# A GRU over 200 steps: gathers of 127 rows with single-row fetches beside them, and a softmax for each chain

## What is computed

```python
x = emb[item_seq]                     # 512 x 200 x 128, f32
def step(h, (x_t, m_t)):              # 200 steps
    mx = x_t @ W + b_i                # 128 -> 3*128
    mh = h @ U + b_r
    z = sigmoid(mx[:, :D] + mh[:, :D])
    r = sigmoid(mx[:, D:2*D] + mh[:, D:2*D])
    hh = tanh(mx[:, 2*D:] + r * mh[:, 2*D:])
    return where(m_t, z * h + (1 - z) * hh, h)
out = softmax(h_last @ Wout + bout)
```

## Time and profile before

| | us |
|---|---|
| median of 3 runs | 1042.61 (1042.57 to 1042.8) |
| profiled execution: span | 1043.0 |
| profiled execution: its own time | 1044.85 |
| PE, DVE, ACT, POOL busy | 975.0, 794.0, 593.0, 765.2 |
| table gathers, L356: count, mean | 738, 0.946 |
| single-row DMAs, L275: count | 1792 |

### The profile page before, as it was taken

One profiled execution on the slowest core, in us unless ns is written; L12 is line 12 of the kernel. 1 busy time (PEld: TensorE's weight loads), 2 busy tenths in 40 slices (PEclk: granted clock), 3 DMA queues, 4 the chain that ended last, 5 costly groups with the idle time before them and its releaser, 6 DMA issues.

```text
span 1043.0 us, 20057 instructions
## 1 busy us (share of the span) xinstructions
PE 975.0 (93%) x5201; PEld 758.8 (73%) x5201; DVE 794.0 (76%) x2074; ACT 593.0 (57%) x1292; POOL 765.2 (73%) x807
## 2 busy tenths in 40 slices
PE   6899999999999999999999999898888988989885
PEld 4556888777777777777777777676666766767664
DVE  3344667888888888888888888777777777777775
ACT  2334555666666666666666666555555555555553
POOL 6576777777777777777777777777777777777772
PEclk9999999999999999999999999999999999999998
DMA  9999555555555555555555555555555555555552
GB/s 357 404 355 282 162 162 159 160 163 160 162 161 160 160 160 161 161 162 161 159 162 159 161 161 161 160 159 162 159 161 162 159 159 161 159 161 160 162 160 71
DMA packets 63942, 184.75 MB, mean 177 GB/s; under 512 B 18207, under 2 KB 21577, under 8 KB 63914
## 3 DMA queue, kind: packets, MB, share of 16 engines
q0 software_dynamic: 48768, 148.29, 50.4%
q1 hardware_dynamic: 13750, 35.24, 9.1%
q10 hardware_dynamic: 1396, 0.91, 0.3%
HBM read 158.31 MB, written 26.08 MB: 177 GB/s over the span
## 4 chain that ended last, share of the span: by engine, by line
PE 53%; POOL 28%; issue 10%; DVE 3%; DMA 3%; ACT 2%; SPq 1%; DVEq 0%; POOLq 0%; ACTq 0%
POOL arena L356 28%; PE bank L443 13%; PE bank L449 9%; PE bank L445 9%; PE bank L431 8%; PE bank L372 5%; PE bank L437 4%; DMA rows<-turned 2%; PE bank L412 1%; PE bank L413 1%; PE bank L417 1%; ACT cand L547 1%; DVE h L610 1%; DVE rh L605 1%; DVE pre L614 1%
## 5 line engine op out<-in xcount | busy, mean ns | idle before, releaser
L356 POOL DMA_INDIRECT arena<-table,row_table x738 | 698.0, 946 | 228.1 <-issue 220.4
L545 ACT ACTIVATE bank<-bank,b_gates 128x256 f32<-128x256 f32 x400 | 179.2, 448 | 252.4 <-PE bank L449 252.4
L431 PE MATMUL bank<-ident,arena 128*128 128x128 f32 x1504 | 254.4, 278 | 44.4 <-DMA arena<-table,row_table 42.7
L431 PEld LDWEIGHTS bank<-ident,arena 128*128 128x128 f32 x1504 | 185.8, 141 | 113.2 <-DMA arena<-table,row_table 74.9
L443 PE MATMUL bank<-h,U_sb 128*128 128x256 f32 x800 | 264.6, 412 | 1.1 <-DVE h L610 1.1
L620 DVE SCALAR_TENSOR_TENSOR bank<-bank,cand 128x256 f32<-128x256 f32 x400 | 172.8, 432 | 121.4 <-ACT cand L547 118.7
L547 ACT ACTIVATE cand<-pre,bi 128x256 f32<-128x256 f32 x400 | 202.9, 507 | 85.9 <-DVE pre L614 85.9
L449 PE MATMUL bank<-h,U_sb 128*128 128x256 f32 x800 | 240.5, 383 | 0.0
L605 DVE SCALAR_TENSOR_TENSOR rh<-bank,br,r 128x256 f32<-128x256 f32 x400 | 193.4, 484 | 60.2 <-ACT r L543 53.2
L445 PE MATMUL bank<-h,U_sb 128*128 128x256 f32 x800 | 238.4, 380 | 0.0
L543 ACT ACTIVATE r<-bank,b_gates 128x256 f32<-128x256 f32 x400 | 189.7, 474 | 36.4 <-PE bank L443 31.9
(11 more groups left out here) (58 smaller groups left out, 236.3 us busy)
## 6 DMA issues: line engine op xcount, KB each, us to landing
arena<-table SPq DMA_DIRECT2D x1792, 1.5 KB
table<-proj SPq DMA_DIRECT2D x24, 768.0 KB, 4.0
arena<-table,row_table POOLq DMA_INDIRECT x738, 3.1
arena<-in_L_rec_emb SPq DMA_DIRECT2D x12, 512.0 KB, 9.9
rows<-turned SPq DMA_DIRECT2D x12, 512.0 KB, 10.2
raw<-rows,row_table POOLq DMA_INDIRECT x48, 4.3
seq<-in_r_item_seq ACTq DMA_DIRECT2D x1, 400.0 KB, 8.0
table<-proj SPq DMA_DIRECT2D x2, 192.0 KB
```

Source lines behind the costliest of these rows:

```text
L356: pool.indirect_dma_start(ring_rows(s, k), None, table, bass.IndirectOffsetOnAxis(row_table[:, t, k:k + 1], 0)).then_inc(s_slot[s][k], 16)
L431: pe.matmul(dst[:, i * P:(i + 1) * P], ring_row(s, k, g), ident[:, :], start=(i == 0), stop=False, is_transpose=True, skip_group_check=True)
L545: act.activation(update_sum[c], update_sum[c], ACT.Sigmoid, bias=b_gates[:, 0:1]).then_inc(s_z[c], 1)
```

## The change

There are two parts. **The gathers.** POOL now gathers all 56 blocks of a turn, but of each only the rows of partitions 0 to 126 (752 gathers of 127 rows instead of 738 of 128). SP fetches the row of partition 127 of each block and step with a DMA of its own, four for each step: 752 single-row DMAs instead of 1792. Their offsets need no way through DRAM any more: POOL writes `row_offsets` for all steps and blocks, and SP loads the 28 of half a turn from partition 127 of it. SP waits for both chains to free the slot. PE waits, before the first transpose of each chain, for the four rows of the step as well (`s_last_row[s]`). The raw gathers stay at 128 rows. **The softmax.** It runs for each chain by itself: the bias is added by PE (identity times `bout_sb`, ahead of the wait for h), DVE takes the negated maximum of a chain, ACT computes exp with it as bias and adds up the total as it goes, one instruction per block, DVE inverts and multiplies, and SP stores the two halves apart.

```diff
-            def slow_block(turn):
-                for first in range(0, P, BATCH_ROWS):
...
-                        if isinstance(turn, int):
-                            sp.wait_ge(s_slot[SLOW_STEP][SLOW_BLOCK], 16)
-                        else:
-                            sp.wait_ge(s_free[1], (turn - 1) * RING + SLOW_STEP + 1)
-                    for i in range(BATCH_ROWS):
-                        p = first + i
-                        sp.dma_start(slot[p:p + 1, :], table_bytes[:, bass.ds(offset[i], ROW_BYTES)]
-                                     ).then_inc(s_slow, 16)
+            def last_rows(turn, steps):
+                for half in range(2):
+                    n = steps // 2
                     _, offset = nc.values_load_multi_w_load_instructions(
...
+                        row_offsets[P - 1:P, bass.ds((turn * RING + half * n) * BLOCKS, n * BLOCKS)],
...
+                    for i in range(n):
+                        s = half * n + i
+                        if not isinstance(turn, int) or turn > 0:
+                            for c in BOTH:
+                                sp.wait_ge(s_free[c], (turn - 1) * RING + s + 1)
+                        for k in range(BLOCKS):
+                            sp.dma_start(ring_rows(s, k)[P - 1:P, :].bitcast(U8),
+                                         table_bytes[:, bass.ds(offset[i * BLOCKS + k], ROW_BYTES)]
+                                         ).then_inc(s_last_row[s], 16)
...
                     for k in CHAINS[c]:
-                        if (s, k) == (SLOW_STEP, SLOW_BLOCK):
-                            continue
                         if n < RAW:
                             pool.wait_ge(s_slot[n][k], 16)
                         pool.indirect_dma_start(
-                            ring_rows(s, k), None, table,
-                            bass.IndirectOffsetOnAxis(row_table[:, t, k:k + 1], 0)
+                            ring_rows(s, k)[0:P - 1, :], None, table,
+                            bass.IndirectOffsetOnAxis(row_table[0:P - 1, t, k:k + 1], 0)
                         ).then_inc(s_slot[s][k], 16)
...
-                        if n == 0 and (s, k) == (SLOW_STEP, SLOW_BLOCK):
-                            pe.wait_ge(s_slow, (turn + 1) * (P * 16))
-                        elif n == 0:
+                        if n == 0:
+                            if i == 0:
+                                pe.wait_ge(s_last_row[s], (turn + 1) * (BLOCKS * 16))
                             pe.wait_ge(s_slot[s][k], turn * 16 + (32 if s < RAW else 16))
...
             for c in BOTH:
+                for i in range(2):
+                    pe.matmul(logits[c][:, i * CLASSES:(i + 1) * CLASSES], ident[:, :], bout_sb[:, :],
+                              start=(i == 0), stop=False, skip_group_check=True)
                 pe.wait_ge(s_h[c], STEPS + 1)
...
+            for c in BOTH:
+                act.wait_ge(s_top[c], 1)
+                for i, k in enumerate(CHAINS[c]):
+                    act.activation(exps[:, k, :], logits[c][:, i * CLASSES:(i + 1) * CLASSES], ACT.Exp,
+                                   bias=minus_top[:, k:k + 1], accum_out=total[:, k:k + 1]).then_inc(s_exp[c], 1)
...
+            for c in BOTH:
+                first, end = CHAINS[c][0], CHAINS[c][-1] + 1
+                dve.wait_ge(s_logit_ps[c], 1)
+                dve.tensor_reduce(minus_top[:, first:end], logits[c].rearrange("p (k n) -> p k n", k=2),
+                                  AX.X, ALU.max, negate=True).then_inc(s_top[c], 1)
+            for c in BOTH:
+                first, end = CHAINS[c][0], CHAINS[c][-1] + 1
+                dve.wait_ge(s_exp[c], 2)
+                dve.reciprocal(inv_total[:, first:end], total[:, first:end]).then_inc(s_inv[c], 1)
+                dve.wait_ge(s_inv[c], 1)
+                dve.tensor_tensor(probs[:, first:end, :], exps[:, first:end, :],
+                                  inv_total[:, first:end].unsqueeze(2).to_broadcast([P, 2, CLASSES]), ALU.mult
+                                  ).then_inc(s_prob[c], 1)
```

More of the change, by code:

```diff
@@ L53, in gru @@
     LEFT = STEPS - RAW - TURNS * RING
-    assert SLOW_STEP < min(RAW, LEFT)
+    assert RING % 2 == 0 and LEFT % 2 == 0 and RING * BLOCKS // 2 <= 32
     BOTH = range(len(CHAINS))
@@ L112, in gru @@
         row_table = sb("row_table", [P, STEPS, BLOCKS], I32)
-        slow_offsets = sb("slow_offsets", [P, TURNS + 1], I32)
-        slow_line = sb("slow_line", [1, (TURNS + 1) * P], I32)
+        row_offsets = sb("row_offsets", [P, (STEPS - RAW) * BLOCKS], I32)
         copy_i = sb("copy_i", [P, 1], I32)
@@ L135, in gru @@
         zh = chain_tiles("zh")
-        logits = sb("logits", [P, BLOCKS, CLASSES])
         exps = sb("exps", [P, BLOCKS, CLASSES])
-        top = sb("top", [P, BLOCKS])
+        probs = sb("probs", [P, BLOCKS, CLASSES])
+        minus_top = sb("minus_top", [P, BLOCKS])
         total = sb("total", [P, BLOCKS])
@@ L148, in gru @@
         x_sum = [bank[4 * c + 3][:, 0:WIDTH] for c in BOTH]
-        logit_bank = bank[3]
+        logits = [bank[4 * c + 3][:, 0:2 * CLASSES] for c in BOTH]
         turn_bank = bank[0:4]
@@ L176, in gru @@
         s_slot = [[sem(f"slot{s}_block{k}_gathered") for k in range(BLOCKS)] for s in range(RING)]
[L177 to L180, removed]
+        s_offsets = sem("row_offsets_ready")
+        s_last_row = [sem(f"slot{s}_last_rows_fetched") for s in range(RING)]
         s_x = per_chain("x_turned")
@@ L194, in gru @@
         s_h = per_chain("h_ready")
[L195 to L198, removed]
+        s_logit_ps = per_chain("logits_summed")
+        s_top = per_chain("tops_ready")
+        s_exp = per_chain("exp_ready")
+        s_inv = per_chain("totals_inverted")
+        s_prob = per_chain("probs_ready")
         s_out = sem("out_stored")
@@ L245, in _ @@
             sp.dma_start(table[ITEMS + 1:ITEMS + 1 + P, :], last[:, 2, :]).then_inc(s_last, 16)
[L249 to L254, removed]
             for q in range(AHEAD):
@@ L257, in _ @@
             sp.wait_ge(s_padrow, 16 * 2)
-            sp.wait_ge(s_slow_line, 16)
-            slot = ring_rows(SLOW_STEP, SLOW_BLOCK).bitcast(U8)
-            def slow_block(turn):
-                for first in range(0, P, BATCH_ROWS):
+            sp.wait_ge(s_offsets, 1)
+            def last_rows(turn, steps):
+                for half in range(2):
+                    n = steps // 2
                     _, offset = nc.values_load_multi_w_load_instructions(
-                        slow_line[0:1, bass.ds(turn * P + first, BATCH_ROWS)], engines=[sp.engine],
-                        min_val=0, max_val=(ITEMS + P) * ROW_BYTES,
+                        row_offsets[P - 1:P, bass.ds((turn * RING + half * n) * BLOCKS, n * BLOCKS)],
+                        engines=[sp.engine], min_val=0, max_val=(ITEMS + P) * ROW_BYTES,
@@ L286, in _ @@
+            last_rows(0, RING)
+            with sp.Fori(1, TURNS) as turn:
+                last_rows(turn, RING)
+            last_rows(TURNS, LEFT)
+            for c in BOTH:
+                first, end = CHAINS[c][0], CHAINS[c][-1] + 1
+                sp.wait_ge(s_prob[c], 1)
+                sp.dma_start(out[first * P:end * P, :].rearrange("(k p) n -> p k n", p=P),
+                             probs[:, first:end, :]).then_inc(s_out, 16)
+            sp.wait_ge(s_out, 16 * len(CHAINS))
         @block.gpsimd
@@ L323, in _ @@
             pool.wait_ge(s_idx, 7)
-            pool.tensor_scalar(slow_offsets[:, :], row_f[:, SLOW_BLOCK, RAW + SLOW_STEP:STEPS:RING],
+            pool.tensor_scalar(row_offsets[:, :].rearrange("p (t k) -> p t k", k=BLOCKS),
+                               row_f.rearrange("p k t -> p t k")[:, RAW:STEPS, :],
                                float(ROW_BYTES), None, ALU.mult).then_inc(s_offsets, 1)
@@ L495, in _ @@
             for c in BOTH:
+                for i in range(2):
+                    pe.matmul(logits[c][:, i * CLASSES:(i + 1) * CLASSES], ident[:, :], bout_sb[:, :],
+                              start=(i == 0), stop=False, skip_group_check=True)
                 pe.wait_ge(s_h[c], STEPS + 1)
[L497 to L501, removed]
+                for i in range(2):
+                    last = pe.matmul(logits[c][:, i * CLASSES:(i + 1) * CLASSES], h[c][:, i * P:(i + 1) * P],
+                                     Wout_sb[:, :], start=False, stop=True, skip_group_check=True)
+                last.then_inc(s_logit_ps[c], 1)
         @block.scalar
@@ L563, in _ @@
             over_table_steps(act, one_turn)
-            act.wait_ge(s_soft, 3)
-            act.activation(exps[:, :, :], logits[:, :, :], ACT.Exp).then_inc(s_exp, 1)
+            for c in BOTH:
[3 more added lines that the diff above has]
+                                   bias=minus_top[:, k:k + 1], accum_out=total[:, k:k + 1]).then_inc(s_exp[c], 1)
         @block.vector
```

5 lines of the change are left out of this document (removed).

## The result

The changed kernel takes **2260.88 us** (median of 4 runs, 2260.15 to 2262.68) where the kernel before takes 1042.7: a ratio of 2.168, 95% interval 2.165 to 2.171. The forecast was 996.4, the range 990 to 1060. The direction and the size are both wrong.

A forecast was written before the change was run, and what follows sets the result against it. The prediction took POOL's gather stream to bound the kernel before, and PE the changed one: 1043.0 - 44.2 (PE's pace) - 2.0 (softmax) = 996.8 us of span, less 0.4 = 996.4 us; range 990 to 1060.

The forecast's parts named there:

- What bounds the kernel: PE sets the pace until about 640 us, then POOL's gather stream does, 1.2507 us from start to start.
- D: Forecast case: gathers get cheap enough that PE's own pace bounds the kernel, 996.4 us; chance 59%.
- rival B: Gathers on one engine at unchanged generation cost, the longer landing on the path: 1063 to 1068 us; chance 7%.
- Part 1: One more POOL gather per turn, 752 for 738: 17.5 us at the old price, all on the path.
- the offsets' way through DRAM: SP's two offset DMAs through DRAM go; SP had time there, gain 0.
- Part 2: POOL's gathers of 127 rows for 128: generation below 0.87 us, bounds 0.06 to 0.939 us, far end 1.21.
- Part 3: With PE as the bound at 2.186 us per slot, the span falls by 44.2 us to 998.8.
- the 44 us: Span saved once PE's own pace sets the end: 44.2 us.
- SP's single rows and the added wait: SP's row fetches cost 0; PE's new waits per step taken as 0, kept at 0 to 8 us.
- POOL's larger table of offsets: Table grown to 128x752 elements takes 1.6 to 2.9 us, hidden behind 9.55 us of POOL idling: cost 0.
- Part 4: Softmax per chain after the last h: 1.7 us left of 3.80, gain 2.0 us, 1.6 if the sum lengthens exp.
- A: Cost is per row or engines stay sixteen; POOL remains the bound: 1052.6 to 1058.1 us; chance 20%.

The follow-up runs named there:

- 112-row run: The changed kernel with 112 rows instead of 127 in POOL's gathers, SP's single rows and the waits kept, rows 112 to 126 left out: 1038.22 us, ratio 0.9961.
- the ladder: The changed kernel without SP's fetches and PE's wait for them, POOL's gathers at another row count each turn, from 128 to 32: 1303.4 us.

## Why the prediction was wrong

**What bounds the kernel: right for the kernel before, wrong for the changed one.** I had PE take over (D); POOL's stream stayed the bound. From the first table gather to the last plus a tail it gave every span that I computed within 1%, except that of the 112-row run (1.2%). With the measured 2.845 us from start to start, the forecast's own sum for POOL, 102.86 + 751 x 2.845 + 16.4, is 2255.9 us, 2266 with rival B's 10 us for the longer landing; the span was 2260.8.

**Part 1, right in kind, less in size.** I said 17.5 us for the 14 gathers. The runs with all 128 rows and with the softmax alone differ by just this part of the change: 1054.16 - 1039.94 = 14.2 us, 14.0 in the two profiled spans. Three things take the 17.5 down. The fourteenth gather is that of the very last block, behind the gather that PE waits for last (the seventh before the last with the softmax alone, the eighth with all 128 rows), so only 13 gathers lengthen the path: 1.25 us less, a mistake of my sum. POOL's pace up to that gather was 1.2500 us and not 1.2519: 1.4 us. And 1.5 us is that the first table gather starts earlier (100.95 against 102.49 us); the gather waited for last landed 0.7 us later instead. The earlier start is the item that I had costed at nothing: the offsets' way through DRAM. In the three kernels that keep it the first table gather starts at 102.5 to 103.2 us, in the five without it at 100.3 to 101.0. In the three POOL waits there for the table's stores, 2.2 to 3.7 us. That the way through DRAM delays the end of these stores, by its 1,792 pieces of 4 B, is argued and not shown.

**Part 2 is the step that failed, and the whole of the error.** I took two shares of a gather's 0.946 us that could shrink, per row and per engine, and concluded that one engine instead of sixteen can only make it cheaper. The bounds ran from 0.06 to 0.946 us, with 1.21 as a remote end. The true cost is a third thing, the waves: n/k times an entry for *all* sixteen engines. I had the right fact in hand, that 127 divides by nothing, and the right consequence for the transfer: one engine per gather, landing at "about 13 us", measured 12.8. But the same packets of the earlier trace rows fit "eight waves of sixteen" just as well as "sixteen engines of eight rows", and nothing in them excluded that the number of waves, which goes from 8 to 127, carries the price. The upper bound of an operation that the trace does not show was set where the known form stands; a form that splits differently could cost more, and I gave that no row and no chance. The 119 further waves cost 119 x 13.1 ns = 1.56 us and the step from k = 16 to k = 1 another 0.03: 1.60 us per gather, 1.2 ms in all. My sentence on the Trainium skill's rule ("DMA: Bandwidth & Descriptors", "Why a DMA increments its semaphore by 16 and not by 1") had a hint at the missing half: from GpSimd all 16 engines post the semaphore whatever the shape. I read it as "the cost per engine might stay", never as "times the waves".

**Part 3.** PE's pace without POOL as the bound was not tested; the 44 us stayed unreached. The parts costed at nothing held: SP's single rows and the added wait (112 rows against 128: 15.9 us measured, 15.8 from the gathers alone), and POOL's larger table of offsets (2.78 us in the ladder, behind which POOL still idles 5.5 us).

**Part 4.** 2.0 us said, 2.0 measured on the chain from h to the last product, plus 0.8 for the halved store, which I had missed. The reading of the sum, 0.19 us, is real; the first of chain 1's lies beside the second exp, the second stands in front of the reciprocal. The terms were off and made up for each other, which is luck: chain 1's two exps with their readings took 0.76 us (0.34 for an exp) where I had 0.54, and the gaps 0.09 where I had 0.25.

**The rivals.** A had the engine that bounds and the sign, but its price stopped at today's. B was the nearest: one engine, long landing, on the path. It kept 0.946 us for the generation. None of the rivals let the generation grow.

## What to carry to other kernels

The number of rows of an indirect gather is a shape, and its price follows n/k, with k the largest divisor of n up to 16. Keep it a multiple of 16; one row less can cost more than twice. And when a trace does not show a form of an operation, bound its cost on both sides by how the work would be *divided*, not only by how much of it there is: fewer engines can mean more steps. Taking rows off a gather that keeps k = 16 brings little, since by the ladder 0.84 of its 0.947 us do not depend on them (0.865 us at 32 rows, less two waves; 112 rows save 21 ns).

## What the runs showed of the hardware that I had not expected

- A wave of a gather costs POOL 13.1 ns for k under 16 and 0.873 us stand beside it; at k = 16 the same 8 waves are 33 ns cheaper than at k = 15 (0.947 against 0.980 us).
- With k = 1, the fifteen engines without a row are still given some 4 B per row: 530,944 packets in the queue instead of 48,768.
- Landing grows with the rows and the bytes of the one engine: 12.7 us for 127 rows of 1,536 B, 7.4 for 127 of 512 B, 7.6 for 61 of 1,536 B, against 3.1 for 128 rows on sixteen.
- POOL starts a gather every 2.85 us while each lands only 12.8 us after its issue; it was never held back by that: all 752 idle times before a gather are issue.
